# Pair weights stored in 128 rows by GpSimd's queue instead of in 125 rows by SyncE's

## The reference, cut to what matters

```
def _L0_gnn_ref(x, edge_row, edge_col, edge_vals, w, b):
    deg = segment_sum(edge_vals, edge_row);  dinv = deg ** -0.5
    norm_vals = edge_vals * dinv[edge_row] * dinv[edge_col]
    msg = norm_vals[:, None] * (x @ w)[edge_col]
    return relu(segment_sum(msg, edge_row) + b)
...
x = x + _L0_gnn_ref(_layernorm(x), src, dst, edge_weight, L0_gnn_w, L0_gnn_b)
```

## Time and profile before

| what | value |
|---|---|
| median of three runs | 7893.16 us (7884.82 to 7912.25) |
| the profiled execution's own time | 7891.96 us |
| its span | 7889.8 us |
| PE busy over the span | 6118.2 us (78%) |
| PE weight loads (PEld) | 4498.1 us (57%) |
| DVE busy | 4354.1 us (55%) |
| ACT busy | 2977.0 us (38%) |
| POOL busy | 2115.4 us (27%) |
| SyncE's DMA queue (q1) | 381076 packets, 509.18 MB |
| GpSimd's DMA queue (q0) | 156320 packets, 549.61 MB |

### The profile page before, as it was taken

One profiled execution on the slowest core, in us unless ns is written; L12 is line 12 of the kernel. 1 busy time (PEld: TensorE's weight loads), 2 busy tenths in 40 slices (PEclk: granted clock), 3 DMA queues, 4 the chain that ended last, 5 costly groups with the idle time before them and its releaser, 6 DMA issues. The chain is left out here.

```text
span 7889.8 us, 111595 instructions
## 1 busy us (share of the span) xinstructions
PE 6118.2 (78%) x32572; PEld 4498.1 (57%) x32573; DVE 4354.1 (55%) x7888; ACT 2977.0 (38%) x7414; POOL 2115.4 (27%) x2115
## 2 busy tenths in 40 slices
PE   6566666648998877888887595888887599587998
PEld 5265666644555444655554483666665588366666
DVE  7544444420001455888886525999997411786333
ACT  0043443423444234555553231555444332233333
POOL 0000000000000033777773151777774122000000
PEclk9877776769998888999998697999998799788999
DMA  1144444433332057777774243777775332321000
GB/s 38 34 148 149 149 146 149 150 116 103 104 96 62 3 182 279 229 228 229 231 228 104 71 141 118 237 238 234 234 237 142 116 108 97 128 93 39 8 12 20
DMA packets 544416, 1071.07 MB, mean 136 GB/s; under 512 B 71164, under 2 KB 361872, under 8 KB 530487
## 3 DMA queue, kind: packets, MB, share of 16 engines
q0 software_dynamic: 156320, 549.61, 22.9%
q1 hardware_dynamic: 381076, 509.18, 20.2%
q10 hardware_dynamic: 6560, 6.55, 0.3%
HBM read 764.83 MB, written 300.26 MB: 135 GB/s over the span
## 5 line engine op out<-in xcount | busy, mean ns | idle before, releaser
L2185 POOL DMA_INDIRECT rows<-l_kv,index_staged x1708 | 1729.9, 1013 | 707.5 <-issue 493.6
L2298 PE MATMUL sum<-messages,hot 128*128 128x260 f32 (+1 forms) x3416 | 955.4, 409 | 52.8 <-issue 24.2
L2274 PE MATMUL q<-queries,spread 128*128 x5136 | 716.0, 286 | 132.3 <-DVE rows L2435 85.9
L2244 ACT ACTIVATE messages<-rows,messages 128x64 f32<-128x64 f32 (+1 forms) x3392 | 774.3, 323 | 0.0
L2298 PEld LDWEIGHTS sum<-messages,hot 128*128 128x128 f32 x3416 | 607.0, 195 | 156.1 <-issue 73.3
L2274 PEld LDWEIGHTS q<-queries,spread 128*128 128x128 bf16 x5136 | 488.4, 101 | 324.4 <-issue 218.8
L2435 DVE TENSOR_TENSOR rows<-q,rows 128x512 f32<-128x512 f32 x854 | 573.0, 683 | 148.9 <-DMA rows<-l_kv,index_staged 147.3
L588 DVE TENSOR_TENSOR hot_lane<-lanes_b,unit_lane 128x1920 bf16<-128x1920 bf16 x97 | 209.4, 2158 | 660.9 <-PE weight_window L608 660.8
L2441 DVE TENSOR_REDUCE sc<-rows 128x32 f32<-128x2048 f32 (+1 forms) x214 | 487.4, 2279 | 1.8
L639 PEld LDWEIGHTS weight_window<-lane_f,key_w 128*125 128x125 f32 x2910 | 480.9, 260 | 0.1
L639 PE MATMUL weight_window<-lane_f,key_w 128*125 128x128 f32 x2910 | 480.9, 342 | 0.0
(11 more groups left out here) (532 smaller groups left out, 11404.4 us busy)
## 6 DMA issues: line engine op xcount, KB each, us to landing
edge_counts<-count_stage SPq DMA_DIRECT2D x32, 2875.0 KB
pair_weights<-weight_stage SPq DMA_DIRECT2D x32, 2875.0 KB
rel<-slot_rel SPq DMA_DIRECT2D x218, 256.0 KB
counts<-edge_counts SPq DMA_DIRECT2D x8, 4800.0 KB
first_part<-in_L_ffn_first SPq DMA_DIRECT2D x32, 1030.0 KB
pairs<-pair_weights SPq DMA_DIRECT2D x250, 125.0 KB
rows<-l_kv,index_staged POOLq DMA_INDIRECT x1708
edge_attr<-in_attr SPq DMA_DIRECT2D x124, 208.0 KB
```

The source lines that it names most:

```text
L2185: pool.indirect_dma_start(out=rows[:, u * 2 + n, j, :], out_offset=None, in_=table, in_offset=bass.IndirectOffsetOnAxis(ap=staged[:, u, n ...
L2244: act.activation(messages[:, 1, j, h, 0:HD], rows[:, u * 2 + 1, j, D + h * HD:D + (h + 1) * HD], ACT.Copy, scale=messages[:, 1, j, h, HD:H ...
L2274: ins = pe.matmul(q_ps[g % QUERY_BANKS][:, r, :], spread[:, t[1] * 2 + n, g * RUN % U + r, :], qs[:, bass.ds(tile, 1), m, :], start=m == 0 ...
L2298: ins = pe.matmul(sum_ps[g % 2][:, 0:W], hot[:, n, j, :], messages[:, n, j, :, :].rearrange("p h d -> p (h d)"), start=r == 0, stop=r == R ...
```

## The change

`pair_weights` gets 128 rows instead of 125, the store takes all 128 rows of `weight_stage` (rows 125 to 127 were cleared at the start and stay zero), and it is issued by GpSimd's queue. GpSimd loads the offset of the group itself and waits for `weight_kept` and `weights_stored` itself; SyncE keeps the counts only. The reader takes rows 0 to 124 as before.

```
-    k.pair_weights = nc.dram_tensor("pair_weights", [C, GROUP_SLOTS, P], F32, kind="Internal").ap()
+    k.pair_weights = nc.dram_tensor("pair_weights", [P, GROUP_SLOTS, P], F32, kind="Internal").ap()
...
             @block.gpsimd
             def _(pool):
                 pool.memset(none[:, :], 0.0).then_inc(made, 1)
                 pool.memset(count_stage[:, :, :, :], 0.0).then_inc(made, 1)
+                reg = pool.alloc_register(ph._name("block_group"))
+                for b in range(BLOCKS):
+                    last = min(WINDOWS, (b + 1) * BLOCK_WINDOWS)
+                    slots = (last - b * BLOCK_WINDOWS - 1) * U + W
+                    pool.reg_load(reg, bases[0:1, b, 1:2])
+                    pool.wait_ge(weight_kept, last)
+                    if b:
+                        pool.wait_ge(weights_stored, 16 * b)
+                    at = nc.snap(reg, min_val=0, max_val=GROUP_SLOTS - slots)
+                    pool.dma_start(k.pair_weights[:, bass.ds(at, slots), :],
+                                   weight_stage[:, b % 2, 0:slots * P].rearrange("p (g c) -> p g c", c=P)
+                                   ).then_inc(weights_stored, 16)
+                pool.wait_ge(weights_stored, 16 * BLOCKS)
...
             @block.sync
             def _(sp):
-                regs = [sp.alloc_register(ph._name(f"block_base{n}")) for n in range(2)]
+                reg = sp.alloc_register(ph._name("block_base"))
...
-                    sp.reg_load(regs, bases[0:1, b, :])
+                    sp.reg_load(reg, bases[0:1, b, 0:1])
...
-                    sp.wait_ge(weight_kept, last)
-                    if b:
-                        sp.wait_ge(weights_stored, 16 * b)
-                    at = nc.snap(regs[1], min_val=0, max_val=GROUP_SLOTS - slots)
-                    sp.dma_start(k.pair_weights[:, bass.ds(at, slots), :],
-                                 weight_stage[0:C, b % 2, 0:slots * P].rearrange("p (g c) -> p g c", c=P)
-                                 ).then_inc(weights_stored, 16)
...
-        weights = k.pair_weights.rearrange("(n t) g c -> n t g c", n=E)
+        weights = k.pair_weights[0:PAIR_ROWS, :, :].rearrange("(n t) g c -> n t g c", n=E)
```

More of the change, by code:

```diff
@@ L684, in _ @@
                         sp.wait_ge(counts_stored, 16 * b)
-                    at = nc.snap(regs[0], min_val=0, max_val=(GROUP_SLOTS - slots) * E)
+                    at = nc.snap(reg, min_val=0, max_val=(GROUP_SLOTS - slots) * E)
                     sp.dma_start(k.counts[:, :, bass.ds(at, slots * E)], count_stage[:, b % 2, :, 0:slots * E]
                                  ).then_inc(counts_stored, 16)
-                    sp.wait_ge(weight_kept, last)
-                    if b:
-                        sp.wait_ge(weights_stored, 16 * b)
-                    at = nc.snap(regs[1], min_val=0, max_val=GROUP_SLOTS - slots)
-                    sp.dma_start(k.pair_weights[:, bass.ds(at, slots), :],
-                                 weight_stage[0:C, b % 2, 0:slots * P].rearrange("p (g c) -> p g c", c=P)
-                                 ).then_inc(weights_stored, 16)
                 sp.wait_ge(counts_stored, 16 * BLOCKS)
-                sp.wait_ge(weights_stored, 16 * BLOCKS)
 def split(step, dve, value, rest, parts):
```

## The result

The changed kernel took 7833.03 us (median of 4 runs, 7826.97 to 7838.64), the one before 7894.24 us beside it. The ratio is 0.9921, with a 95% interval of 0.9906 to 0.9936: 61 us or 0.8% faster, in the range given, 19 us under the time predicted. The profiled execution took 7836.03 us with a span of 7834.4 us, 55.4 us less than the span before.

What follows compares the result with a forecast made beforehand. PE and its gaps behind the load of 17 registers were taken to set the stage. The terms -26.6 - 8.6 + 0 + 12 - 18 gave -41 us, 7852 beside the median; 8 in 10 range 7790 to 7980.

Steps and rivals of the forecast that it cites:

- gaps at t0+22 to +26: PE's gaps before windows, 22 to 26 us after a counts store starts (t0): down to 2.0 us, 26.6 us off.
- their windows: PE's windows behind the gaps at t0+22 to +26: become those behind a 2.0 us gap, 8.6 us off.
- gaps at t0+16: PE's gaps begun 16 us after the counts store starts: no change taken, bounds -18 and +50 us.
- gaps in the full phase: PE's 10 us gaps while all DMA engines are busy: as long as now plus 0.5 us each, +12 us.
- the end: Last weights store of the stage, which landed at 1693.4: lands sooner, 18 us off (16 to 22).
- waits for "issue": PE's summed gaps ahead of the first matmul of windows: 413 us before, near 398 us after the change.
- 128 rows use all engines, and they are idle from t0+19: Stores of each block: all 16 engines full to about t0+18 to +22, then idle, not a third until t0+34.
- The full phase governs the gap: Rival, PE's gaps: PE goes on only when both stores are drained, +147 us, 8039; chance 0.11.
- Counts and weights share each engine: Rival, DMA engines: serve both stores in turn, holding up the counts; gaps 3 us longer, +19, 7912; chance 0.24.
- GpSimd issues 5888 pieces: Rival, weights store: rows not joined, 46.6 us of issue per store, +450 us, 8340; chance 0.04.
- The queue at no cost: Weights store issued by GpSimd instead of SyncE: 128 pieces would cost 1 us beside PE's gap, nothing in the sum.

Runs made afterwards that it cites:

- rows128_sp: The kernel before with only the 128 rows, the weights store staying on SyncE's queue: 7836.29 us, ratio 0.9927 to the kernel before.
- weights_late: The changed kernel with the weights store held back until PE has loaded the registers of the second window behind it: 7785.07 us, ratio 0.9866 to the kernel before.
- rows125_pool: The changed kernel with 125 rows again, so only the move to GpSimd's queue is left: 7987.54 us, ratio 1.0113 to the kernel before.
- six_registers: The changed kernel with 6 instead of 17 registers loaded per window, products of units 4 to 14 going to places of units 0 to 3: 7432.68 us, ratio 0.9412.
- packed: The changed kernel with five four-bit places per word, so PE loads 5 registers and unpacks by arithmetic: 7530.67 us on a quicker chip, ratio 0.9639 to the kernel before.

## Why the prediction was right, point by point

| term | predicted | measured |
|---|---|---|
| gaps at t0+22 to +26 | -26.6 | -30.6 (8 x 1.41 + 8 x 2.41) |
| their windows | -8.6 | -5.0 |
| gaps at t0+16 | 0 | -9.2, and +5.4 in their windows |
| gaps in the full phase | +12 | +5.3, and +4.8 in their windows |
| other gaps | 0 | -7.4, and +5.3 in their windows |
| the end | -18 | -15.8 |
| outside the stage | 0 | -7.4 |
| sum | -41 | -55.4 by the spans (-54.6 by the terms) |

The forecast gave the waits for "issue" as 398 us; they are 371. The gaps fell by 42 us instead of 15, and the windows took 10 of them back instead of giving 9 more. So the stage came out near the forecast in part because two errors stood against each other.

- **128 rows use all engines, and they are idle from t0+19**: this is shown by the changed profile, and rows128_sp shows that it is the active part.
- **Gaps at t0+22 to +26 fall to idle ones**: this was right in mechanism and size.
- **Gaps at t0+16**: "I take no change" was off by 9 us. They begin 3 us before the traffic ends and end with it; their last loads have quiet time, as in weights_late.
- **The full phase**: the number was right, 10.76 us, which is luck in part, for the reason was only half so. I held that a gap's length does not hang on the traffic behind it. weights_late and rows125_pool say that it does, through the rate at which loads are served: the gap is 7 to 8 us with the counts alone, 10.8 with the 128 rows behind them, 16.4 with the 125 rows of GpSimd's queue. It stayed at its old value because the traffic up to t0+11 is the same, and behind that the loads are served hardly more slowly beside the weights on all engines than beside those on five.
- **The rivals**: "The full phase governs the gap" failed because a gap ends when its loads are served, some 4 to 7 us before the traffic does. "Counts and weights share each engine" failed because they don't: the weights' first packet starts when the counts are all but through, and on average less than 1% of the counts' packets start behind t0+12. rows128_sp, with one queue, has the same gaps. The prediction said that the trace before has no stretch with both queues; that is so in this stage, not in the whole trace. "GpSimd issues 5888 pieces" failed because the rows are joined: a store is 128 packets, and its issue takes 0.53 us.
- **Clock**: the windows behind the gaps at t0+22 to +26 gained 5 us, and the others lost 16, those behind shortened gaps among them (windows 1, 2, 5, 11). With gaps of 1 to 10 us a window mostly takes 9 to 10 us, and one without a gap 6.6. The term was too regular a reading of small differences.
- **The end**: it was -15.8 against -18, as worked out.
- **The queue at no cost**: this is shown by the equal times of rows128_sp and the changed kernel. The sentence of the Trainium skill in "DMA: Bandwidth & Descriptors", "Issuing engines are not separate DMA queues", agrees with that. It does not hold for 125 rows, where the queue alone made some 90 us: 135 GB/s on a third of the engines from SyncE, 236 GB/s on all of them from GpSimd.
- **Outside the stage**: it was 3.7 us before the stage, where both kernels run the same instructions, and 3.7 behind it. That is variation between executions (the first window begins anywhere from 368.3 to 372.5 us in the eleven profiles), and half of the 14 us by which the sum missed.

## What to carry to other kernels

A transfer that nobody waits for can still cost time through a sequencer that loads registers beside it. Here a block's traffic ended 15 us sooner and the kernel gained under 2 us per block, since the loads of only some windows had met the part that went away. So look at what runs when the transfer does. Before tuning a store, count the registers that an engine loads per step, and pack them or time the store behind them; here that was worth another 3.9% (0.9536 against 0.9921), five times the change itself. Give a store rows in a number that fills the DMA engines, and don't take 125 for nearly 128.

## What the runs showed of the hardware that I had not expected

- A register load from SBUF costs PE 0.83 us in dense DMA traffic (loads 7 to 17 of a batch, six_registers against the changed kernel); 17 of them leave PE idle for about 2 us in quiet time, and 6 for none.
- Two stores run one behind the other, on two queues as on one. With nothing before it, a weights store of GpSimd's has its first packet 1.1 us behind its issue (weights_late); behind the counts it comes only at t0+11.1, some 4.5 us behind the issue (the changed kernel).
- A store of 125 rows takes a third of the engines and 135 GB/s from SyncE's queue, and all of them at 236 GB/s from GpSimd's; with 128 rows GpSimd's gives 381 GB/s, and the store ends at about t0+19 from either queue.
- Register arithmetic on PE shows between short products: 0.06 us more for each of the 15 count products of a window ((2.5 - 1.6) / 15), in packed against the changed kernel.
- Left open: each fourth window has no gap in idle time or light traffic, and 2 us in full traffic, in all kernels with 17 loads in a batch. No run here explains it.
